# A hybrid layer kernel on one core: gathered rows of three tiles in the ring instead of two

## The reference

```
c_kv = x @ W_dkv
q_i = (x @ idx_wq).reshape(B_, L_, N_IDX_HEAD, D_HEAD)
k_i = x @ idx_wk
I = jnp.einsum('bths,h->bts', relu(einsum('bthd,bsd->bths', q_i, k_i)), idx_w)
I = jnp.where(local[None], jnp.inf, I)         # the last 64 keys always count
I = jnp.where(causal[None], -jnp.inf, I)
_, idx = jax.lax.top_k(I, 96)
key_c, value = rows idx of c_kv @ W_uk and c_kv @ W_uv      # 8 heads
key_r = _pope(kr_sel, angles_k)                # rotated by rank in the selection
scores = (q_c . key_c + q_r . key_r) * scale
out = softmax(scores) @ value
```

## Time and profile before

| | |
|---|---|
| median of 3 runs | 1296.28 us (1295.68 to 1298.57) |
| the profiled execution | 1299.49 us, span of its instructions 1297.6 us |
| mean granted TensorE clock | 0.851 |
| PE busy | 1041.3 us (80%) |
| DVE busy | 789.7 us (61%) |
| ACT busy | 705.2 us (54%) |
| POOL busy | 574.3 us (44%) |
| gathers (L791) | 496, busy 480.0 us |

### The profile page before, as it was taken

The page is one execution under the profiler, slowest core; times in us unless marked ns, Lnnn a source line. Parts: engine busy times, 40 slices in busy tenths (PEclk is TensorE's granted clock), DMA queues, the critical chain, the costliest instruction groups (busy, mean ns, idle before and its releaser), DMA issues. The chain is left out here.

```text
span 1297.6 us, 20533 instructions
## 1 busy us (share of the span) xinstructions
PE 1041.3 (80%) x7234; PEld 786.3 (61%) x7234; DVE 789.7 (61%) x1468; ACT 705.2 (54%) x1928; POOL 574.3 (44%) x614
## 2 busy tenths in 40 slices
PE   8999999999865887786887878777887774819886
PEld 6888676675533565564666655656665563608744
DVE  5888765756554776675676565566665572603346
ACT  6776554646354646555755574455564552515645
POOL 0210342433563656666666566565565626261001
PEclk9999999999885868778876898788888786858989
DMA  7000000000163242241231221212212202021000
GB/s 224 4 18 2 7 31 1 1 1 1 30 145 77 67 104 53 66 119 34 64 91 47 58 60 33 53 34 59 57 32 59 61 15 61 12 60 42 1 1 32
DMA packets 58740, 62.12 MB, mean 48 GB/s; under 512 B 27760, under 2 KB 43152, under 8 KB 58256
## 3 DMA queue, kind: packets, MB, share of 16 engines
q1 hardware_dynamic: 42768, 36.41, 10.7%
q0 software_dynamic: 15872, 24.41, 9.0%
HBM read 52.65 MB, written 8.13 MB: 47 GB/s over the span
## 5 line engine op out<-in xcount | busy, mean ns | idle before, releaser
L791 POOL DMA_INDIRECT gathered_rows<-key_table,idx_T x496 | 480.0, 968 | 359.0 <-issue 125.6
L835 PE MATMUL bank<-gate_w 128*128 128x384 f32 x384 | 166.4, 491 | 64.4 <-issue 25.9
L2418 DVE TENSOR_TENSOR turned_rows<-bank,rank_rope 96x512 f32<-96x512 f32 x128 | 87.5, 684 | 191.2 <-remote 87.7
L1900 ACT ACTIVATE attn_out<-bank 32x128 f32<-32x128 f32 x128 | 33.6, 263 | 240.6 <-remote 158.0
L835 PEld LDWEIGHTS bank<-gate_w 128*128 128x128 f32 x384 | 85.1, 228 | 121.2 <-issue 93.5
L2392 DVE SCALAR_TENSOR_TENSOR index_sums<-index_relu,iw,index_sums 128x512 f32<-128x512 f32 (+4 forms) x114 | 76.2, 669 | 101.4 <-ACT index_relu L1854 64.4
L835 PE MATMUL bank<-probs_window,local_values 80*32 80x128 f32 x256 | 58.7, 317 | 67.9 <-issue 37.3
L1300 PE MATMUL bank<-ident,gathered_rows 128*96 128x128 f32 x512 | 93.0, 311 | 18.8 <-DVE turned_rows L2418 15.4
L835 PE MATMUL bank<-index_k_hi,index_q 128*128 128x512 f32 (+5 forms) x160 | 81.9, 515 | 22.5 <-DVE idx_T L2412 7.8
L1854 ACT ACTIVATE index_relu<-bank 128x512 f32<-128x512 f32 (+4 forms) x152 | 75.1, 508 | 42.2 <-remote 19.3
L1300 PEld LDWEIGHTS bank<-ident,gathered_rows 128*96 128x96 f32 x512 | 66.7, 145 | 25.1 <-issue 21.5
(11 more groups left out here) (302 smaller groups left out, 2573.1 us busy)
## 6 DMA issues: line engine op xcount, KB each, us to landing
queries_in<-q_rot SPq DMA_DIRECT2D x32, 256.0 KB
gathered_rows<-key_table,idx_T POOLq DMA_INDIRECT x496
q_rot<-rotated SPq DMA_DIRECT2D x16, 256.0 KB
queries_in<-q_lat SPq DMA_DIRECT2D x16, 256.0 KB
h<-in_h SPq DMA_DIRECT2D x2, 1024.0 KB, 8.0
q_lat<-q_latent_sb SPq DMA_DIRECT2D x8, 256.0 KB
local_values<-key_table SPq DMA_DIRECT2D x15, 80.0 KB
rope_tables<-in_cos_ql SPq DMA_DIRECT2D x4, 256.0 KB
```

The source lines that it names most:

```text
L791: pool.indirect_dma_start(out=G[i % 2][:, gather_place(i, q), :], out_offset=None, in_=key_table[0:index_width(i), :], in_offset=bass.Indi ...
L835: return pe.matmul(out_, lhsT, rhs, start=start, stop=stop, **kw)
L2418: v.tensor_tensor(GT[n % 2].rearrange("r (j p) -> r j p", j=4), bank[2][0:ROW, :].rearrange("r (j p) -> r j p", j=4), rank_rope[:].unsquee ...
```

## The change

The ring of gathered rows gets a third buffer, `gathered_rows2`. Tile i uses buffer i modulo 3, and POOL waits before a group for the values of the same group three tiles back instead of two. The first tile with such a wait is tile 3. The 12 KB for it come from the descriptor scratch, which becomes 4 KB of each partition (a launch parameter). Semaphores are scarce, so buffers 1 and 2 get one for two groups: their groups 2k and 2k + 1 are waited for together. Buffer 0 keeps one for each group.

```
-        G = [over("gathered_rows0", [P // QD, ROW]), None]
+        G = [over("gathered_rows0", [P // QD, ROW]), None, sb("gathered_rows2", [P, P // QD, ROW])]
...
-            return (q + FIXED // QD) % (P // QD) if i % 2 == 0 else q
+            return (q + FIXED // QD) % (P // QD) if i % RINGS == 0 else q
...
-        gathered = [[sem(f"gathered{b}_{g}") for g in range(NG)] for b in range(2)]
+        GROUPS_SIGNALLED = (1, 2, 2)
+        gathered = [[sem(f"gathered{b}_{g}") for g in range(NG // GROUPS_SIGNALLED[b])] for b in range(RINGS)]
...
-                    out=G[i % 2][:, gather_place(i, q), :], out_offset=None, in_=key_table[0:index_width(i), :],
+                    out=G[i % RINGS][:, gather_place(i, q), :], out_offset=None, in_=key_table[0:index_width(i), :],
...
-                ).then_inc(gathered[i % 2][q // (GQ // QD)], 16)
+                ).then_inc(gathered[i % RINGS][q // (GQ // QD) // GROUPS_SIGNALLED[i % RINGS]], 16)
...
-                    if i >= 2 and q % (GQ // QD) == 0:
-                        pool.wait_ge(a_pv, NG * (i - 2) + q // (GQ // QD) + 1)
+                    if i >= RINGS and q % (GQ // QD) == 0:
+                        pool.wait_ge(a_pv, NG * (i - RINGS) + q // (GQ // QD) + 1)
...
-                    gathers = i // 2 + (i % 2 == 1 or g >= FIXED // GQ)
-                    pe.wait_ge(gathered[i % 2][g], 16 * GQ // QD * gathers)
+                    gathers, together = i // RINGS + (i % RINGS > 0 or g >= FIXED // GQ), GROUPS_SIGNALLED[i % RINGS]
+                    pe.wait_ge(gathered[i % RINGS][g // together], 16 * GQ // QD * together * gathers)
...
-    nc = bacc.Bacc("TRN2", target_bir_lowering=False, num_devices=1)
+    nc = bacc.Bacc("TRN2", target_bir_lowering=False, num_devices=1, dynamic_dma_scratch_size=4096)
```

More of the change, by code:

```diff
@@ L258, in place @@
             return nc.alloc_sbuf_tensor_at(name, [parts, *shape], dt, offset=offset)[:]
-        RING = 2 * C
+        RING, RINGS = 2 * C, 3
         k_lo = place("index_k_lo", early_offset, [T], F32R)
@@ L1299, in rows_turn @@
                 for j in range(4):
-                    last = pe.transpose(bank[2][0:ROW, j * P:(j + 1) * P], G[i % 2][:, gather_place(i, 4 * g + j), :], ident[:])
+                    last = pe.transpose(bank[2][0:ROW, j * P:(j + 1) * P], G[i % RINGS][:, gather_place(i, 4 * g + j), :], ident[:])
                 last.then_inc(a_gt, 1)
@@ L1343, in values @@
                 for j in range(4):
-                    last = mm(o_[:, j * w:(j + 1) * w], G[b][:, gather_place(i, g * 4 + j), 2 * DR:ROW],
+                    last = mm(o_[:, j * w:(j + 1) * w], G[i % RINGS][:, gather_place(i, g * 4 + j), 2 * DR:ROW],
                               PTg[n % 2][:, j * w:(j + 1) * w], False, True, skip_group_check=True)
```

## The result

The changed kernel takes 1385.62 us (median of 6 runs, 1381.33 to 1392.41), the kernel before in the same comparison 1296.24 us (6 runs, 1289.07 to 1298.57). The ratio is 1.07, its 95% interval 1.0673 to 1.0727. It is 89 us slower, where +34 was forecast, and above the range of 1290 to 1353.

The account below looks back on a forecast made before the run. PE's signals, seen late while POOL gathers back to back, were taken as the bound. Terms 37 + 0 + 5 - 8 = +34 us on 1299.49 gave 1333; that execution being 3.2 us above the median, 1330 us was predicted, range 1290 to 1353.

Parts of the forecast that it names:

- The mechanism: What PE signals is seen late while POOL issues gathers back to back; POOL's old wait for `a_pv` brakes it.
- a tile's gathers take 45 us and let 3 slots by: Price of gathering a tile's 32 rows with buffers already free, read from tiles 14 and 15: 6 slots in 45.2 + 44.9 us.
- A: Slots 4 to 12: tile 2 and five groups of tile 3 gathered unpaced, 90.5 against 54 us, +37 (+19 to +45).
- D: Slots 83 to the end: tiles 13 to 15 gathered unpaced, with free slots between, -8 us (-15 to 0 in the forecast range).
- B: Slots 12 to 76: POOL stays paced, one tile further ahead, at the same 6.4 us a slot; cost 0.
- C: Slots 76 to 83: tile 12's index comes with three groups of tile 9 done; 50 against 45 us, +5.
- The free pace: Time of a slot while POOL has nothing to do: 4.5 us, taken as 4.3 for longer stretches late in the kernel.
- E: Shared signal: PE waits for four gathers more (5 us), hidden by the five slots before a tile's first turn; taken as 0.
- F: Smaller descriptor scratch: 0 us taken, up to 15 if each of the 496 gathers took 0.03 us more.
- The free stretches pay: Faster rival: unpaused gathers let more PE slots by, break-even 6.6 slots, giving 1284 us; chance 0.18.
- No change: Rival: the lag belongs to the work of slots 105 to 116, not to POOL; gathers just move, 1296 us; chance 0.09.
- Much slower: Rival: smaller scratch makes many gathers longer, or unpaused gathers lock more than shown; 1355 us and above; chance 0.07.

## Why the prediction was right in its mechanism and wrong in its size

*The mechanism* was right for the lag chips, and its sign too; that the lag depends on the chip no row of before could show. In the trace's record of semaphore events, the events of ACT and DVE stand within 0.01 us of their instructions; only TensorE's are late, those of the values by up to 24 us before and 34 us after, and after POOL stops at 456.8 those held back come through together, from 457.7 to 462.2, in the order in which they were given. That POOL's unpaused gathers cause it is shown by the two edits to waits alone: old waits in the changed kernel take some 80 us away, and pauses in the late tiles of the kernel before take 25 away. The lower clock of the runs is not the loss: PE's work takes 1041 us in all in both kernels. By the Trainium skill (TensorE: Matmul & The Clock Gate, "The cost: per-tile semaphore tail") the tail behind one matmul with one increment is an estimated 0.06 us, worked out from the page's formula. The record agrees on the no-lag chips and with POOL idle (0.01 to 0.06 us), and differs in a run (up to 34 us); there the measurement decides.

*The step that failed* is "a tile's gathers take 45 us and let 3 slots by". A whole run takes 40 us and lets 1 or 2 by, and then some 5 us more pass before the last of the signals is through. The 3 was the mean of 4 and 2, and the 4 was no run: tile 14's gathers stopped at 1088.76 after 24, waiting for a buffer, and two of its four rotations (at 1094.2 and 1103.3) came behind that gap. In the whole runs of the changed kernel two rotations can lie 30.1 us apart (433.9 and 464.0) and 38.1 (1043.3 and 1081.4); before, the longest such gap in tile 14 was 17.6. I had read both pauses, and then counted the slots as if they belonged to the run. The bound from above (2 slots, as in tile 15's) was the better price. Term by term the sum of A to D was forecast at +34 and is +85; D is the largest miss (22 us), then A (15).

*A, slots 4 to 12*: forecast +37 (19 to 45), measured +52. The run let 2 slots by; the index of tile 3 came at 473.35, 56.9 us after the run's window began, in place of 49.5; and 24 gathers of tile 3 were unpaused where I had 20. The mean granted clock in the stretch was 0.60, with PE busy for 51.5 of 106.0 us, against 0.78 with 44.7 of 53.8.

*B and C, slots 12 to 83*: forecast 0 and +5, measured +18. C is 56.6 us against 43.8 for the same rotations, so +13: tile 12's gathers cost more than I gave them. B is +5.4 (416.0 against 410.6).

*D, slots 83 to the end*: forecast -8, measured +14 (306.0 against 291.7). The free pace was right, 52.60 us for 12 rotations behind tile 13's run, 4.4 us a slot, and the new run of tile 13 paid for itself (+0.3 in its window). What I had left out is that runs 14 and 15 would no longer be cut short: +10.2 and +5.3 us. Before, POOL stopped for a buffer after 24 and 28 gathers; with a third buffer it does not. The prediction had both at the same 45 us as before, so it put this at nothing.

*E, the shared signal*: 0, as forecast. In the trace no wait of PE's turns (L1301) is ended by a gather.

*F, the scratch*: forecast 0 (up to 15), measured +17 by itself on one lag chip, nothing (ratio 0.9956) on a no-lag one. Its place was wrong too: gathers are not longer. In the changed kernel it can't be told from the buffer; with old waits both cost 12 us. A to D are measured in windows, so they hold whatever there is of it.

*The rivals.* "The free stretches pay" needed 6.6 slots in a run and got 1 or 2; the kernel with late tiles paced shows the reverse, that it pays to take runs away. "No change" held the lag for a thing of the late slots; tile 2's run in slots 4 to 7 refutes it. "Much slower" (0.07) is the time that came, and half of its mechanism: the runs lock more than shown.

*The signs.* Those named for being right came: tile 2 is gathered from 416.7 to 456.8 without a pause, ACT waits longer on "remote", tile 13's gathers take 40 us, and a gather still takes 0.94 us. But the eighth rotation after the index of tile 2 came at 523.0 and not near 510, and the count in a run was 1 or 2 where 2 to 4 had been named: the same miss in two forms. Two sums in the prediction are off by 3 us: its bounds add up to 1305 from below and not 1308, and D with no gain is -3 and not 0. Neither explains the miss.

*The best version* seen here is the kernel before with the late tiles paced, 0.979 of it, on a lag chip; on a no-lag chip it is the same as before (0.9971).

## What to carry to other kernels

A wait that looks like a shortage (a ring too small by one buffer) can be the pause on which other engines' signals depend: before widening a ring, look in the timeline at how long after its producer's end a consumer starts, with and without the issuing engine at work. When a cost per run is read from two examples, check that they are whole; here both were cut short, and two of the six slots counted came behind the gap. A brake has to be a pause relative to the gathers just issued, since a count that others have already passed brakes nothing.

## What the runs showed of the hardware

- On the lag chips TensorE's semaphore events come up to 34 us late while GpSimd issues indirect DMAs 0.30 us apart, and within 4 to 6 us of its stop all of them are through. ACT's and DVE's don't lag. With rows of 32 bytes they lag as with 384 (31.5 us in one run of gathers).
- The same kernel takes 1296 to 1303 us on some chips and 1066 to 1068 on others, where nothing lags and PE is busy for 90% of the span. Why chips differ in this stays open.
- 4 KB of descriptor scratch in place of 16 made no gather longer (median 0.944 us) and yet cost 1.3% (0.9 to 1.7) on one lag chip, and nothing on a no-lag one (ratio 0.9956).
